# W_in split into twelve blocks, tables of two stages loaded a stage ahead, and four buffers for turned choices

## The chip, the cores and the metric

One core of one Trainium2 chip. The metric is the device time of the kernel in microseconds. A core has TensorE (PE in the profile; its weight loads are PEld), VectorE (DVE), ScalarE (ACT), GpSimd (POOL) and SyncE (SP), which here issues nearly all transfers. The engines run their own instruction streams and meet at semaphores. A transfer that SP issues is worked off by the core's 16 DMA engines.

## What is computed

One layer: a long convolution with a gate and a residual, a layer norm, a layer of experts with a residual, and another layer norm, over 8192 positions of 512 features, in float32.

```python
u = x @ W_in + b_in                       # 8192 x 1536
uc = _short_conv(u, short_w, short_b)     # three taps along the sequence
x0, x1, v = jnp.split(uc, 3, axis=-1)
v = v * x1
k = _gen_filter(...)                      # h = sin(..sin(pe @ W1)..W2), k = (h @ W3 + b3) * decay
v = _causal_fft_conv(v, k, filter_bias)   # length 16384, by Fourier transforms
y = v * x0
x = _layernorm(x + y @ W_out + b_out)
# experts: in each group of 32 positions every expert takes the position with the largest logit
perm = (logits == max over the group)     # logits = x @ controller + tie
inner = relu(x[perm] @ f1 + bias);  out = scatter(inner @ f2)
x = _layernorm(x + out)
```

## The kernel before

The program is four stages, one after the other (`program`, L1534; the list at L1531). Each stage makes its own buffers and semaphores, and its engines start together after the engines of the stage before have all ended; SP ends a stage by waiting for all of that stage's stores (L244 to L248, L643, L920 to L924), since the next stage reads them from memory.

A product that must be exact to float32 is made of three products: each operand is split into a high part (a cast to float32r, `split_high`, L77) and a low part (the rest, `split_low`, L82), and `product` (L87) multiplies high with high, low with high and high with low. W_in, x, W3, the filter's spectrum, y and W_out are treated so.

**Front stage** (`front_phase`, L113). x is worked in 17 groups along the sequence: a halo group of 256 columns (group 0), then 16 of 512. For each group TensorE runs twelve units (`unit`, L261), one for each block of 128 of the 1536 columns of W_in, in the order x0, x1, v of feature block 0, then of block 1, and so on (`w = x % 3 * DT + x // 3`). A unit is twelve matmuls into one of three PSUM buffers. ACT copies a unit's end as the halo of the next group (`keep_halo`, L350) and applies the third tap (`tap`, L357), DVE adds the other taps (`taps_add`, L465), gates and damps v (`gate`, L484) and makes the filter's angles (`angles`, L448); TensorE turns v (L280) and transforms it along one axis (`stage`, L287) in between. SP's queue begins with the whole of W_in (L193, 3 MB), the halo group of x (L194), six constants (L195 to L200), twelve parameters of the filter (L203 to L206), four position and transform tables (L209, L210), and the second group of x (L211), for which it waits until x's first split is done. ACT splits W_in in four instructions (L394), then x (L396); DVE makes W_in's low part in four (L427), POOL x's (L252). TensorE waits for all four low parts of W_in (L320), runs group 0, then waits for the constants and the parameters (L323, L324) and runs the other groups.

**Frequency stage** (`frequency_phase`, L524), 64 pairs of rows. SP loads nine tables (L614 to L623), then pairs 0 to 3 (`load`, L589), then writes the split table of ones to memory as six stores (L628) and reads it back a pair at a time (`load_ones`, L599, two pairs ahead). For each pair TensorE transforms v (L650) two pairs ahead, the filter's basis (L661) one pair ahead, makes the filter (L672) and the inverse (L684) of the pair two behind. DVE multiplies, POOL adds, ACT copies. TensorE begins when four tables are there (L648), its first filter when W3 is split (L703).

**Output stage** (`output_phase`, L787), 64 tiles of 128 positions. SP loads tile 0 (z and its transform, x0), then eight tables (L900 to L908, W_out among them), x of tile 0, and tiles 1 and 2. All of TensorE, ACT, DVE and POOL wait for the eight tables (L941, L1002, L1062, L929), then ACT and DVE split W_out (L1043, L1119), for which TensorE waits (L986). A tile is a convolution's last step (`conv`, L943), the gate, the product with W_out (`out`, L954), the norm, and the logits of 128 experts' slots (L970). At the end comes a tail: DVE marks the chosen positions in eight units (`choose`, L1108), TensorE turns them in sixteen (`turn_take`, L977), ACT writes each turned unit twice with a mask, once for each of two sides (`keep_took`, L1028), into one of two buffers, and SP stores sixteen of those (TOOK) and eight of the unturned (TAKE, L887).

**Experts' stage** (`experts_phase`, L1136): not touched.

## Time and profile before

| | us |
|---|---|
| device time, median of three runs | 2304.3 (2299.67 to 2306.85) |
| own time of the profiled execution | 2312.54 |
| its span | 2310.7 |
| TensorE busy | 1933.4 (84% of the span) |
| DVE, ACT, POOL busy | 1387.6, 949.0, 440.1 |
| moved by the DMA engines | 522.65 MB, 226 GB/s |

The profile is of one execution, which took 2312.54 us; it has the span from the first to the last instruction, and all times in it are counted from the span's start. The stages begin at about 2, 784, 1154 and 1613 us. A busy share is an average over stages with different limits, so it says little by itself. "Idle before" is time in which an engine stood ahead of an instruction, with what ended it.

### The profile page before, as it was taken

Reading aid. Unit: us, or ns where it says so; the run is one execution under the profiler, and the core shown is the slowest. Engines: PE = TensorE matmul, PEld = TensorE weight load, DVE = VectorE, ACT = ScalarE, POOL = GpSimd, SP = SyncE. Lnnn points to the kernel's source line nnn. Section 1 sums busy time; section 2 is a strip of 40 time slices with the busy share of each in tenths; the row PEclk is TensorE's granted clock in tenths of the full one; section 3 lists DMA queues with packets and bytes.
Section 4 is the critical chain, followed back from the end, with each engine's and each line's share of the span. In section 5 each row is a group of like instructions: output and inputs, shape, how many; then the busy total and the mean of one; then the engine's idle time right before and its main releaser. Section 6 shows DMA issues by size and latency. Waiting matters only on the chain. (4 is left out here: it accounts for less than half of the span.)

```text
span 2310.7 us, 35055 instructions
## 1 busy us (share of the span) xinstructions
PE 1933.4 (84%) x12598; PEld 1322.0 (57%) x12598; DVE 1387.6 (60%) x2672; ACT 949.0 (41%) x1756; POOL 440.1 (19%) x279
## 2 busy tenths in 40 slices
PE   5999999999999699999769999994767676576444
PEld 5777777777777344444359988883636362252000
DVE  3878777777777255555458888882443354354344
ACT  3444444444444344444345555554323232242222
POOL 1100010011000044444345554540000000000000
PEclk9999999999999799999979999996888887686655
DMA  4134233423332578888587777756797999989999
GB/s 144 65 110 136 102 110 110 142 101 110 117 130 92 174 202 222 221 220 223 160 258 239 243 245 225 238 185 240 251 398 270 393 345 407 406 302 409 372 392 341
DMA packets 300365, 522.65 MB, mean 226 GB/s; under 512 B 26943, under 2 KB 119263, under 8 KB 291874
## 3 DMA queue, kind: packets, MB, share of 16 engines
q1 hardware_dynamic: 290978, 503.63, 64.5%
q10 hardware_dynamic: 9216, 16.78, 1.9%
q8 instruction: 103, 1.69, 0.3%
q14 instruction: 68, 0.56, 0.1%
HBM read 314.50 MB, written 205.82 MB: 225 GB/s over the span
## 5 line engine op out<-in xcount | busy, mean ns | idle before, releaser
L89 PE MATMUL p_pu<-p_xT_high,p_win_high 128*128 128x512 f32 (+1 forms) x816 | 334.6, 410 | 23.7 <-POOL p_xT_low L84 23.5
L91 PE MATMUL p_pu<-p_xT_low,p_win_high 128*128 128x512 f32 (+1 forms) x816 | 318.3, 390 | 0.0
L90 PE MATMUL p_pu<-p_xT_high,p_win_low 128*128 128x512 f32 (+1 forms) x816 | 318.3, 390 | 0.0
L369 ACT ACTIVATE p_t<-p_pu,p_tbias,p_taps 128x512 f32<-128x512 f32 x192 | 149.4, 778 | 385.2 <-PE p_pu L91 384.1
L473 DVE SCALAR_TENSOR_TENSOR p_t<-p_halo,p_taps,p_t 128x128 f32<-128x128 f32 (+1 forms) x384 | 196.8, 517 | 137.0 <-ACT p_t L369 135.9
L473 DVE SCALAR_TENSOR_TENSOR p_t<-p_pu,p_taps,p_t 128x384 f32<-128x384 f32 (+1 forms) x384 | 210.2, 547 | 6.9
L751 POOL TENSOR_TENSOR q_y<-q_y 128x512 f32<-128x512 f32 x128 | 160.3, 1273 | 277.8 <-DVE q_y L778 277.8
L84 POOL TENSOR_TENSOR p_xT_low<-p_xT,p_xT_high 128x2048 fp32r<-128x2048 f32 (+1 forms) x17 | 77.2, 4541 | 626.0 <-ACT p_xT_high L79 626.0
L89 PEld LDWEIGHTS p_pu<-p_xT_high,p_win_high 128*128 128x128 f32 x816 | 155.0, 190 | 56.9 <-issue 29.4
L1427 DVE COPY e_taken<-e_pd 128x1024 f32<-128x1024 f32 x64 | 78.4, 1224 | 161.8 <-PE e_pd L1360 161.6
L91 PEld LDWEIGHTS p_pu<-p_xT_low,p_win_high 128*128 128x128 f32 x816 | 154.4, 189 | 34.6
L1372 PE MATMUL e_pd<-e_taken,e_ff 128*32 128x128 f32 x2048 | 90.0, 333 | 96.6 <-DMA e_ff<-in_L_ffn_f 93.0
L90 PEld LDWEIGHTS p_pu<-p_xT_high,p_win_low 128*128 128x128 f32 x816 | 155.1, 190 | 27.5
L778 DVE TENSOR_TENSOR q_y<-q_pg,q_v 128x512 f32<-128x512 f32 x256 | 157.9, 673 | 1.9 <-PE q_pg L682 1.8
L1372 PEld LDWEIGHTS e_pd<-e_taken,e_ff 128*32 128x32 f32 x2048 | 67.2, 133 | 159.8 <-DMA e_ff<-in_L_ffn_f 146.3
L1360 PE MATMUL e_pd<-e_pick,e_out 64*128 64x128 f32 x1536 | 111.0, 310 | 56.8 <-DMA e_out<-s_X 30.4
L950 PE MATMUL o_pc<-o_idft,o_zin 128*128 128x128 f32 x1024 | 127.2, 279 | 26.1 <-DVE o_wout_low L84 26.1
L1360 PEld LDWEIGHTS e_pd<-e_pick,e_out 64*128 64x128 f32 x1536 | 107.0, 222 | 66.8 <-issue 34.0
L1434 ACT COPY e_out<-e_pd 128x1024 f32<-128x1024 f32 x64 | 64.7, 1011 | 192.6 <-PE e_pd L1384 192.6
L657 PE MATMUL q_pv<-q_av,q_fwd 128*64 128x512 f32 x512 | 126.3, 616 | 15.7 <-DMA q_ah<-s_SH 15.7
L950 PEld LDWEIGHTS o_pc<-o_idft,o_zin 128*128 128x128 f32 x1024 | 122.0, 195 | 27.0 <-issue 26.9
L296 PE MATMUL p_ps<-p_vt,p_dft 128*128 128x512 f32 x256 | 134.6, 608 | 0.7 <-ACT p_vt L379 0.7
(120 smaller groups left out, 3499.9 us busy)
## 6 DMA issues: line engine op xcount, KB each, us to landing
s_I<-e_out SPq DMA_DIRECT2D x64, 1024.0 KB, 8.2
s_SV<-p_sout SPq DMA_DIRECT2D x128, 256.0 KB, 2.0
q_av<-s_SV SPq DMA_DIRECT2D x64, 512.0 KB, 4.3
s_Z<-q_z SPq DMA_DIRECT2D x128, 256.0 KB, 3.2
o_zin<-s_Z SPq DMA_DIRECT2D x64, 512.0 KB, 3.6
e_ff<-in_L_ffn_f SPq DMA_DIRECT2D x64, 512.0 KB, 8.9
e_inter<-s_I SPq DMA_DIRECT2D x32, 1024.0 KB, 12.8
e_taken<-s_I SPq DMA_DIRECT2D x32, 1024.0 KB, 11.3
```

What stands on the lines that cost most here:

```text
L89: pe.matmul(out, a[0], b[0], start=start, stop=False)
L90: pe.matmul(out, a[1], b[0], start=False, stop=False)
L91: return pe.matmul(out, a[0], b[1], start=False, stop=stop)
L296: pe.matmul(pz[n % 2][:], dft[i % 2][:, j, r, :], vt[i % 2][:, j, :], start=True, stop=True).then_inc(s_ps, 1)
L369: nc.scalar.activation(t[r][m % 2][:], pu[(W + n) % 3][:], ACT.Identity, bias=tbias[:, w:w + 1], scale=taps[:, w, 2:3]).then_inc(t_ok, 1)
L473: return dve.scalar_tensor_tensor(T[:, c], src, taps[:, w, tap:tap + 1], T[:, c], ALU.mult, ALU.add)
L657: m = pe.matmul(pv[r][a * B:(a + 1) * B, :], fwd[:, 1 if 2 * p + a else 0, r * B:(r + 1) * B], av[s][:, a, :], start=True, stop=True)
L751: pool.tensor_tensor(y[p % NY][:, r, :], y[p % NY][:, r, :], y2[p % NT2][:, r, :], (ALU.subtract, ALU.add)[r]).then_inc(y_ok, 1)
L778: dve.tensor_tensor(into, pg[k % NG][:], v[p % NV][:, half, :], ALU.mult).then_inc(g_used, 1)
L950: m = pe.matmul(pc[n % 2][:, k, :], zin[s][:, r, k * P:(k + 1) * P], idft[s][:, r, :], start=(r == 0), stop=(r == 1))
L1360: m = pe.matmul(pd[:, b, h, k].rearrange("p e g -> p g e"), x[r, a, k * P:(k + 1) * P], chosen[r, a, :].rearrange("p (g e) -> p g e", g=2) ...
L1372: m = pe.matmul(ph[s][r, :], ff[w][:, 0, k * P + e * EF:k * P + (e + 1) * EF], rows[:, k, 4 * i + e, :], start=(k == 0), stop=(k == DT - 1))
```

## The change

- `front_tables` and `output_tables` are new: buffers that live over two stages. `program` opens the first ahead of the front stage and the second ahead of the frequency stage, and hands them on.
- W_in is loaded as twelve blocks of 128 columns, in the order of the units, behind the halo group of x; the second group of x follows, then all that stood before. ACT and DVE split it block by block, ACT four blocks ahead of the halo it copies; each unit of group 0 waits for its own block's low part. The unsplit blocks share their memory with a halo buffer and the two buffers of turned v.
- The nine tables of the frequency stage are loaded in the front stage ahead of its main loop, split by ACT in group 14 and by DVE in group 15; the ones are stored by SP after its work of group 15. The frequency stage starts with pair 0 and the ones of pair 0.
- The eight tables of the output stage are loaded in the frequency stage after pair 16; ACT makes W_out's high part in four pieces at pairs 32 to 35, POOL its low part at pairs 33 to 36. The output stage starts with its tiles and waits for no table.
- Turned choices have four buffers. ACT writes the one side, DVE the other (each has a semaphore), DVE between its `choose` instructions.

The diff, cut:

```diff
@@ front_phase @@
+        shared = sb("shared", [P, W * HC + 2 * J * D])
+        halo = [sb("halo0", [P, W, HC])[:], shared[:, 0:W * HC].rearrange("p (w c) -> p w c", w=W)]
+        vt = [shared[:, W * HC + s * J * D:W * HC + (s + 1) * J * D].rearrange("p (j d) -> p j d", j=J) for s in range(2)]
+        win = [shared[:, x * DT * P:(x + 1) * DT * P].rearrange("p (k c) -> p k c", k=DT) for x in range(W)]
...
-            sp.dma_start(win[:], A["W_in"].rearrange("(k p) w -> p k w", p=P)).then_inc(w_in, 16)
+            wd = A["W_in"].rearrange("(k p) w -> p k w", p=P)
             load_x(0)
+            for x in range(W):
+                sp.dma_start(win[x], wd[:, :, at(x)]).then_inc(w_in[x], 16)
+            load_x(1)
             sp.dma_start(taps[:], A["short_w"].rearrange("(w p) k -> p w k", p=P)).then_inc(consts, 16)
...
-            load_x(1)
+            sp.dma_start(ones[:], A["ones"]).then_inc(fw_in, 16)
+            for r in range(2):
+                sp.dma_start(w_raw[0][r * HID:(r + 1) * HID, :], A["W3"]).then_inc(fw_in, 16)
...
+            sp.dma_start(F["fwd"][:], A["fwd"]).then_inc(carried, 16)
...
+                if i == NCH - 1:
+                    sp.wait_ge(ones_low, ONE + 1)
+                    for n, part in enumerate((0, 0, 1)):
+                        for a in range(2):
+                            sp.dma_start(S["ONES"][n, :, :, a, :], F["ones"][part][a * HID:(a + 1) * HID].bitcast(F32)
+                                         .rearrange("p (r b) -> p r b", r=3)).then_inc(ones_st, 16)
...
+                if g == 0:
+                    pe.wait_ge(w_low, ONE + x + 1)
...
-            pe.wait_ge(w_low, ONE + DT)
...
-            act.wait_ge(w_in, ONE + 16)
-            for c in range(DT):
-                split_high(nc.scalar.copy, win_s[0][:, c, :], win[:, c, :]).then_inc(w_high, 1)
+            def high_w(x):
+                act.wait_ge(w_in[x], ONE + 16)
+                split_high(nc.scalar.copy, win_s[0][:, :, at(x)], win[x]).then_inc(w_high, 1)
+
             high(0)
+            for x in range(4):
+                high_w(x)
             for x in range(W):
                 if x == 6:
                     high(1)
+                if x + 4 < W:
+                    high_w(x + 4)
...
             for i in range(NCH + 1):
+                if i == NCH - 2:
+                    act.wait_ge(fw_in, ONE + 80)
+                    split_high(nc.scalar.copy, F["ones"][0][:], ones[:]).then_inc(ones_high, 1)
+                    split_high(nc.scalar.copy, F["w_a"][:], w_raw[0][:]).then_inc(fw_high, 1)
+                    split_high(nc.scalar.copy, F["w_b"][:], w_raw[1][0:HID + 3, :]).then_inc(fw_high, 1)
@@ frequency_phase @@
-            for p in range(NA):
+            for p in range(2):
                 load(p)
-            sp.wait_ge(ones_high, ONE + 1)
-            sp.wait_ge(ones_ok, ONE + 1)
...
+                load_ones(p)
+            for p in range(2, NA):
+                load(p)
...
+                if p == PAIRS // 4:
+                    sp.dma_start(wout[:], A["W_out"].rearrange("(k p) d -> p k d", p=P)).then_inc(w_in, 16)
+                    sp.dma_start(O["grow"][:], A["grow"]).then_inc(carried, 16)
...
             for p in range(-2, PAIRS + LAG):
+                if PAIRS // 2 <= p < PAIRS // 2 + DT:
+                    k = p - PAIRS // 2
+                    act.wait_ge(w_in, ONE + 16)
+                    split_high(nc.scalar.copy, O["wout"][0][:, k, :], wout[:, k, :]).then_inc(w_high, 1)
...
             for p in range(PAIRS):
+                if PAIRS // 2 < p <= PAIRS // 2 + DT:
+                    k = p - PAIRS // 2 - 1
+                    pool.wait_ge(w_high, ONE + k + 1)
+                    split_low(pool, O["wout"][1][:, k, :], wout[:, k, :], O["wout"][0][:, k, :]).then_inc(w_low, 1)
@@ output_phase @@
-            pe.wait_ge(consts, ONE + 16 * NCONST)
...
-            pe.wait_ge(w_low, ONE + 1)
...
+            def keep_took(v):
+                dve.wait_ge(took_ok[0], ONE + v + 1)
+                if v >= NK:
+                    dve.wait_ge(took_st[v % NK], ONE + v // NK * 16)
+                dve.tensor_scalar(took[v % NK][:, :, :, 1, :], pt[v % 2][:].rearrange("p b (h e) -> p b h e", h=2),
+                                  side[:, 1:2], None, ALU.mult).then_inc(took_ok[1], 1)
...
                 for u in chosen(n):
                     choose(u)
+                    if u > UNITS:
+                        for b in range(2):
+                            keep_took(2 * (u - UNITS - 1) + b)
+            for b in range(2):
+                keep_took(2 * UNITS - 2 + b)
```

## Rows read from the trace of the kernel before

**Rows 1.** Windows: stretch, length, busy PE, PEld, DVE, ACT, POOL, PEclk, DMA share, GB/s.

```profile
90.00:700.00 610.00, 610.00 (x2655) 458.93 (x2653) 478.99 (x969) 280.18 (x525) 60.51 (x14) 1.00 0.33 114
...
830.00:1130.00 300.00, 300.00 (x1344) 128.45 (x1342) 156.86 (x280) 143.79 (x280) 140.22 (x112) 1.00 0.81 219
...
1210.00:1370.00 160.00, 160.00 (x1073) 144.40 (x1072) 132.59 (x269) 91.01 (x215) 85.30 (x54) 1.00 0.78 244
```

**Rows 2.** TensorE's waits: us in total, times, longest.

```profile
PE o_pt L983 <- ACT o_took L1033: 15.5, 13, 2.6
```

**Rows 3.** Timeline of the start, all engines: start us, us, engine, line, operation.

```profile
2.36 0.44 SPq L193 DMA_DIRECT2D p_win<-in_L_attn_W_in  x1
...
3.95 8.94 SPq L196 DMA_DIRECT2D p_bin<-in_L_attn_b_in  x1
...
18.36 1.04 ACT L79 CAST p_xT_high<-p_xT 128x1024 fp32r<-128x1024 f32 x1
...
19.48 3.85 POOL L84 TENSOR_TENSOR p_xT_low<-p_xT,p_xT_high 128x1024 fp32r<-128x1024 f32 x1 [19.05 <-ACT p_xT_high L79]
...
21.05 2.31 DVE L432 TENSOR_TENSOR p_tsum<-p_taps 128x12 f32<-128x12 f32 x1
...
23.48 0.55 PE L89 MATMUL p_pu<-p_xT_high,p_win_high 128*128 128x256 f32 x1 [23.48 <-POOL p_xT_low L84]
...
36.77 4.61 POOL L84 TENSOR_TENSOR p_xT_low<-p_xT,p_xT_high 128x2048 fp32r<-128x2048 f32 x1 [13.44 <-ACT p_xT_high L79]
...
45.89 0.78 ACT L369 ACTIVATE p_t<-p_pu,p_tbias,p_taps 128x512 f32<-128x512 f32 x1 [2.49 <-PE p_pu L91]
```

**Rows 4.** Transfers: KB each, median us from issue to landing.

```profile
p_xT<-in_L_attn_xT SPq DMA_DIRECT2D x16, 1024.0 KB, 6.5
...
o_x<-s_X SPq DMA_DIRECT2D x64, 256.0 KB, 4.3
...
q_ones<-in_ones SPq DMA_DIRECT2D x1, 96.0 KB, 2.1
```

**Rows 5.** Timeline of the frequency stage's start.

```profile
784.65 0.33 SPq L614 DMA_DIRECT2D q_ones<-in_ones  x1
...
788.86 0.62 ACT L79 CAST q_w_a<-q_w_raw 128x512 fp32r<-128x512 f32 x1 [1.69 <-DMA q_w_raw<-in_L_attn_b]
...
789.16 0.43 SPq L594 DMA_DIRECT2D q_av<-s_SV  x1
...
790.03 0.69 DVE L84 TENSOR_TENSOR q_w_a<-q_w_raw,q_w_a 64x512 fp32r<-64x512 f32 x1 [2.47 <-ACT q_w_b L79]
...
794.65 6.24 PE L657 MATMUL q_pv<-q_av,q_fwd 128*64 128x512 f32 x16 [15.72 <-DMA q_ah<-s_SH]
```

**Rows 6.** Timeline in the front stage's group 15, DVE and TensorE.

```profile
726.17 1.13 DVE L473 SCALAR_TENSOR_TENSOR p_t<-p_pu,p_taps,p_t 128x384 f32<-128x384 f32 x2
...
730.23 0.58 PE L89 MATMUL p_pu<-p_xT_high,p_win_high 128*128 128x512 f32 x1
```

**Rows 7.** Timeline in the frequency stage, SP and TensorE.

```profile
906.97 1.09 SPq L611 DMA_DIRECT2D s_Z<-q_z  x2
...
908.78 0.92 SPq L594 DMA_DIRECT2D q_av<-s_SV  x1
...
916.51 1.08 PE L657 MATMUL q_pv<-q_av,q_fwd 128*64 128x512 f32 x4
```

**Rows 8.** Timeline of the output stage's start.

```profile
1154.49 0.39 SPq L865 DMA_DIRECT2D o_zin<-s_Z  x1
...
1168.97 1.90 ACT L79 CAST o_wout_high<-o_wout 128x2048 fp32r<-128x2048 f32 x1 [20.50 <-DMA o_ident<-in_ident]
...
1173.48 6.34 PE L950 MATMUL o_pc<-o_idft,o_zin 128*128 128x128 f32 x32 [26.09 <-DVE o_wout_low L84]
```

**Rows 9.** Windows of 3 us in the tail, columns as in rows 1.

```profile
1594.00:1597.00 3.00, 1.09 (x4) 0.72 (x4) 0.00 (x0) 1.74 (x4) 0.00 (x0) 0.50 0.39 140
...
1600.00:1603.00 3.00, 1.49 (x7) 0.79 (x5) 0.00 (x0) 2.12 (x4) 0.00 (x0) 0.50 0.99 373
```

More of the change, by code:

```diff
@@ L814, in output_phase @@
                for s in range(2)]
-        wout_s = [ctx.enter_context(nc.sbuf_tensor(f"o_wout_{n}", [P, DT, D], F32R)) for n in ("high", "low")]
         stats = [sb(f"stats{s}", [P, 6]) for s in range(2)]
@@ L821, in output_phase @@
         top = [sb(f"top{s}", [P, UG]) for s in range(2)]
-        took = [sb(f"took{s}", [P, 4, 2, 2, ES // 2]) for s in range(2)]
-        side = sb("side", [P, 2])
+        took = [sb(f"took{s}", [P, 4, 2, 2, ES // 2]) for s in range(NK)]
         pc = [ps(f"pc{s}", [P, DT, P]) for s in range(2)]
@@ L892, in store_unit @@
                     v = 2 * u + b
-                    sp.wait_ge(took_ok, ONE + v + 1)
-                    sp.dma_start(td[v], took[v % 2][:].rearrange("p b h g e -> p b (h g e)")).then_inc(took_st[v % 2], 16)
+                    for s in range(2):
+                        sp.wait_ge(took_ok[s], ONE + v + 1)
+                    sp.dma_start(td[v], took[v % NK][:].rearrange("p b h g e -> p b (h g e)")).then_inc(took_st[v % NK], 16)
             for n in range(NZ):
@@ L979, in turn_take @@
                 if v >= 2:
-                    pe.wait_ge(took_ok, ONE + v - 1)
+                    for s in range(2):
+                        pe.wait_ge(took_ok[s], ONE + v - 1)
                 for b in range(4):
@@ L1528, in _, with program, run @@
             scale(NT - 1)
-PHASES = [front_phase, frequency_phase, output_phase, experts_phase]
-def program(nc, A, S, phases=None):
-    for phase in phases or PHASES:
+def program(nc, A, S):
+    def run(phase, *tables):
         with ExitStack() as ctx:
-            phase(nc, Semaphores(ctx, nc), A, S)
+            phase(nc, Semaphores(ctx, nc), A, S, *tables)
+    with ExitStack() as made:
+        F = front_tables(made, nc)
+        run(front_phase, F)
+        O = output_tables(made, nc)
+        run(frequency_phase, F, O)
+        run(output_phase, O)
+    run(experts_phase)
 def constants():
```

166 lines of the change are left out of this document (74 added, 92 removed).

## The prediction, made before the changed kernel had run

> **What bounds the kernel now.** I read the windows by stretch first, because the four stages have different limits. In the front stage TensorE is busy for 610.00 of 610.00 us, in the frequency stage for 300.00 of 300.00, in the output stage for 160.00 of 160.00, each at the full granted clock of 2.4 GHz [rows 1]. Whatever starts such a stage earlier moves all that follows; whatever delays TensorE once inside it is lost. The change does not touch the experts' stage, which only starts earlier.
>
> Then TensorE's waits. Three lie ahead of stages, and the rows of the timeline that end them name what came last: 23.48 us at the start, for POOL's low part of x [rows 3]; 15.72 ahead of the frequency stage, for a load [rows 5]; 26.09 ahead of the output stage, for DVE's low part of W_out [rows 8]. A fourth is 15.5 in pieces in the tail, for ACT's copies of turned choices [rows 2]. These the change can reach.
>
> **The change part by part.** Durations are from the one profiled execution: span 2310.7, own time 2312.54 us, which is 8.2 over the median of 2304.3. The sum is a difference and is applied to both.
>
> *1. Start.* Before: x is issued behind the 3 MB of W_in; ACT splits x at 18.36, POOL takes 3.85 more, and the first matmul is at 23.48 [rows 3]. After: x goes first. A small table alone in the queue landed 2.1 us after its issue [rows 4]. The 512 KB of x are 1.7 us more at the 313 GB/s below, and I give a cold queue 0.3: issued at 2.4, it lands at 6.5. ACT's 1.04 ends at 7.6, POOL's 3.85 at 11.4, first matmul at 11.5: **12 us earlier**. If POOL took half of its 4.61 us for 128x2048 [rows 3], it would be 13.5.
>
> Do the twelve blocks keep up? A block has 512-byte rows, as the output stage's loads of x0 have (256 KB, median landing 4.3 us) [rows 4], and that stage moves 244 GB/s at a share of 0.78 [rows 1]: 313 GB/s when full, 0.84 us a block. Block n lands near 6.5+0.84(n+1), the last at 16.6. TensorE needed 19.6 us for the twelve units of the halo group (23.48 to about 43.1, where unit 0 of group 1 begins, 2.8 ahead of its tap at 45.89 [rows 3]), so it asks for the last block after 29. ACT splits block x+4 before it copies halo x, so it is four units ahead.
>
> Group 1 waits for more: x's second group, the six constants and the twelve filter parameters, all now behind W_in in SP's queue. That queue blocks when much is outstanding: before, the issue of b_in hung 8.94 us behind W_in, x and the taps [rows 3]. After: x's second group is issued at 12 (it waits for POOL), lands by 20, and ACT takes it at its sixth halo, near 23; POOL's 4.61 ends by 29.5. The taps are, I estimate, let in at 16 and the other constants by 20; the twelve parameters take 6 us at the 0.5 of a table's issue (nine from 784.65 to 789.16 [rows 5]) and land at 28. TensorE gets there at 11.5+19.6=31.1, 3 us later. I keep 12; the low end is 7, if the queue blocks eight us more.
>
> In the trace DVE's addition of 12 columns takes 2.31 us, just until POOL's split ends [rows 3]. The Trainium skill (SBUF — State Buffer, on the shared port) says that a DVE operation with two SBUF inputs and a GpSimd one shut each other out for a whole instruction. By that, POOL could need only half of 4.61 where DVE is idle; the row agrees, and the start would come 13.5 earlier. I stay at 12, since DVE will be splitting blocks then.
>
> *2. Tables of the frequency stage carried by the front stage.* Nine loads (SP some 4.5 us) stand ahead of the third load of x, which ACT wants 20 us later: nothing. ACT's three splits, at most 0.62 each [rows 5], delay one tap of group 14 by 1.9 us, DVE's three, at most 0.69 [rows 5], the chain of group 15 by 2.1. At the tightest place TensorE starts a unit at 730.23 whose buffer DVE released at 727.30 (726.17+1.13) [rows 6]: 2.9 us of slack, so nothing; without that cover each would cost its 1.9 or 2.1. SP's six stores of ONES (some 4 us of issue) go out in the last group, where TensorE waits for no store.
>
> What it removes: SP issues nine tables (784.65 to 789.16) and then pair 0; TensorE starts at 794.65, 5.5 us after pair 0's issue [rows 5]. After, pair 0 is issued at 784.65: **4.5 us**, and 0.7 more (between 0 and 1.5) for 0.9 MB less ahead of it in the queue: **5.2**. The filters, 9.5 us into the stage, then find ONES landed.
>
> *3. Tables of the output stage loaded at pair 16.* Eight loads, 2.0 MB: 4 us of SP, and 6.8 us of DMA at 300 GB/s, where the share is already 0.81 [rows 1]. In steady state SP stores Z at 906.97 and loads a pair from 908.78 that is first used at 916.51 [rows 7]. Put the store at 0: the batch is issued from 1.7, its packets run from about 4 to 11; the next pair's 640 KB take 2.1 behind it and land at 13.1; they are needed at 9.5. **A loss of 3 us**, once, since TensorE is then late itself and the next pair in time. Bounds: 0, if the queue's gaps absorb it, and 6.8, all of it.
> ACT's four splits of a quarter of 1.90 [rows 8] and POOL's four of a quarter of 4.61 [rows 3] fall one to a pair of 5.4 us, in which both engines are busy for half [rows 1]: nothing, as the inverse wants POOL's result only two pairs later; without that, 1.2 a pair.
>
> *4. Output stage.* SP issues tile 0 at 1154.49 and eight tables behind it; ACT starts at 1168.97 when the last has landed, splits for 1.90, DVE after it, TensorE at 1173.48 [rows 8]. After, the first convolution needs tile 0's 640 KB alone: 1154.5+2.1+2.1+0.3=1159.0: **14.5 us**. Tile 1 is wanted 3.2 later (half of 6.34 [rows 8]) and is 1.2 MB behind, 3.8: up to 0.6 is given back. Bounds 11 and 15.5.
>
> *5. Tail.* Sixteen TOOK and eight TAKE stores, 12.6 MB. A full window runs at 373 GB/s, one at 140 [rows 9]. At 375 the bytes take 33.5 us; now they take some 35.7. Four buffers and two engines remove ACT's waits for stores, not the bytes: 2.2, less 0.7 for the start: **1.5 us**; bounds 0 and 3.
>
> **Sum**: -12 -5.2 +3 -14.5 -1.5 = **-30.2 us**: 2282.3 for the profiled execution, 2274.1 for the median. A difference under 0.3% (7 us) can't be told from none here.
>
> **The rivals.**
> A. The parameters gate group 1. SP's queue stays blocked on the taps' many small descriptors; the 8.94 us of b_in [rows 3] speak for it. The first matmul is at 11.5, but TensorE stands ahead of group 1, and the start gains 6: 2280.1.
> B. The output stage's gap is ruled by transfers. Three tiles of 1.2 MB are wanted at once, and x0 and x of tile 0 lie between tiles. If TensorE gets them no faster than they came before, 8 us are won for 14.5: 2280.6. Against: tile 0 was issued first before too.
> C. The batch at pair 16 starves more pairs than one, as the share of 0.81 leaves little to catch up with [rows 1]: 10 us for 3: 2281.1.
> D. Slower. The twelve blocks don't overlap, and each takes a landing of x0's, 4.3 us [rows 4]. The last lands at 6.5+51.6=58.1, x's second group 6.5 (its median [rows 4]) later at 64.6, ACT and POOL 6.5 more: 71.1 for group 1, against 43.1. That is +28.0 in place of -12, and with the rest's -18.2, 2314.1. It decides from 3.5 us a block on. Against it: 313 GB/s in a stage full of such loads.
> The Trainium skill (DMA: Bandwidth & Descriptors, Anatomy of one DMA) gives each DMA some 2.0 us fixed, and its bytes at 436 GB/s. By that, as an estimate, twelve blocks in a row are 31 us and group 1 begins 7.6 later than now. The tail's stores, one behind the other at 373 GB/s [rows 9], show the fixed parts overlapping.
> E. The tables bring nothing, as each stage first waits for the stores of the one before: only the start gains, 2292.3; or the start fails too, 2304. Against: the waits end on the tables or on what stands behind them [rows 5, 8].
>
> **Chances.** Forecast 0.62; A 0.14; B 0.10; C 0.06; D 0.03; E 0.05, of it 0.03 with no change. All low ends together (7, 4.5, -6.8, 11, 0) give -15.7, 2288.6; all high ends (13.5, 6, 0, 15.5, 3) give -38, 2266.3. So **2265 to 2289** holds the forecast with A, B and C; D and E are left out. Faster by over 0.3%: 0.94; within: 0.03; slower: 0.03.
>
> **What would show it.** First matmul near 11.5, first tap near 34, and no wait of TensorE before the frequency stage. Waits of about 10.5 us ahead of that stage and 11.5 ahead of the output stage, both on a stage's own data. One wait of some 3 us on a pair's load near pair 21. No DMA window with a gap in the tail. A wait of L89 for a constant or for x's second group means A, for blocks of W_in, D; a first convolution later than 4.5 us behind tile 0's issue means B.

## The result, and the profile after

The changed kernel took 2291.82 us (median of five runs, 2287.93 to 2293.73), the kernel before beside it 2305.12 (2299.67 to 2309.86): a ratio of 0.9938, with a 95% interval of 0.9922 to 0.9953, or 13.3 us less. The forecast was 30.2 us less, 2274.1, with a range from 2265 to 2289. The sign was right; the size was not, and the time lies outside of the range. A later comparison of the same two kernels (e_again, below) gave 2295.45 against 2307.09, 0.9950 (0.9937 to 0.9962).

The profiled execution of the changed kernel has a span of 2291.9 and its own time of 2293.73, 18.8 us under the profile of before. The profile of before lay 7.4 us over the median of 2305.12, that of the changed kernel 1.9 over its own, which makes the difference from 13.3. A second profile of the kernel before (e_before, below) has a span of 2303.7. So I read the gain stage by stage.

The windows of the changed kernel, inside the front, frequency and output stages (columns as in [rows 1]):

```profile
90.00:700.00 610.00, 610.00 (x2653) 459.38 (x2653) 479.48 (x963) 282.32 (x528) 64.25 (x14) 1.00 0.33 115
820.00:1120.00 300.00, 294.75 (x1316) 126.34 (x1314) 152.78 (x274) 142.25 (x279) 142.58 (x114) 0.99 0.81 222
1190.00:1350.00 160.00, 160.00 (x1061) 143.64 (x1061) 131.89 (x267) 90.00 (x211) 85.59 (x54) 1.00 0.77 242
```

TensorE still bounds all three. In the middle one it is idle for 5.25 of 300 us, where before it was never idle: that is the batch of tables. The third looks like the row of before and hides a loss, since an engine that is slower and always busy shows no gap.

The timeline of the start, all engines, which answers [rows 3]:

```profile
2.98 0.44 SPq L211 DMA_DIRECT2D p_xT<-in_L_attn_xT  x1
3.48 10.05 SPq L228 DMA_DIRECT2D p_shared<-in_L_attn_W_in  x12
...
8.45 2.35 POOL L84 TENSOR_TENSOR p_xT_low<-p_xT,p_xT_high 128x1024 fp32r<-128x1024 f32 x1 [8.02 <-ACT p_xT_high L79]
...
8.93 4.83 DVE L84 TENSOR_TENSOR p_win_low<-p_shared,p_win_high 128x512 fp32r<-128x512 f32 x5 [5.54 <-ACT p_win_high L79]
...
11.49 0.55 PE L89 MATMUL p_pu<-p_xT_high,p_win_high 128*128 128x256 f32 x1 [11.49 <-DVE p_win_low L84]
...
24.09 4.58 POOL L84 TENSOR_TENSOR p_xT_low<-p_xT,p_xT_high 128x2048 fp32r<-128x2048 f32 x1 [13.29 <-ACT p_xT_high L79]
...
24.56 5.26 DVE L84 TENSOR_TENSOR p_win_low<-p_shared,p_win_high 128x512 fp32r<-128x512 f32 x2 [2.53 <-ACT p_win_high L79]
...
35.27 0.78 ACT L422 ACTIVATE p_t<-p_pu,p_tbias,p_taps 128x512 f32<-128x512 f32 x1 [2.49 <-PE p_pu L91]
```

The first matmul came at 11.49, 12.0 earlier, as forecast; the first tap at 35.27 instead of 45.89, 10.6 earlier. The two rows near 24 say why: DVE's last two blocks took 5.26 us where one alone takes 0.69, for as long as POOL was splitting x's second group, and TensorE waited 1.79 us for the first of them:

```profile
29.27 0.39 PE L89 MATMUL p_pu<-p_xT_high,p_win_high 128*128 128x256 f32 x1 [1.79 <-DVE p_win_low L84]
```

The timeline from the batch at pair 16 on, SP and TensorE (answers [rows 7]), and behind it the windows of the same place:

```profile
876.11 0.99 SPq L691 DMA_DIRECT2D q_wout<-in_L_attn_W_out  x1
...
880.69 0.50 SPq L699 DMA_DIRECT2D t_ident<-in_ident  x1
881.30 0.38 SPq L658 DMA_DIRECT2D q_av<-s_SV  x1
881.72 0.47 SPq L660 DMA_DIRECT2D q_ah<-s_SH  x1
...
889.19 3.40 PE L713 MATMUL q_pv<-q_av,f_fwd 128*64 128x512 f32 x8 [5.25 <-DMA q_ah<-s_SH]
```

```profile
880.00:885.00 5.00, 3.94 (x20) 1.82 (x16) 2.81 (x5) 2.21 (x5) 2.15 (x2) 1.00 0.99 303
885.00:890.00 5.00, 0.81 (x2) 0.30 (x4) 0.00 (x0) 0.04 (x1) 1.29 (x2) 0.88 1.03 375
890.00:895.00 5.00, 5.00 (x20) 2.09 (x18) 1.33 (x3) 1.54 (x3) 0.00 (x0) 0.78 0.64 240
```

One pair's spectra landed at 889.19. TensorE had waited 5.25 us, and ran its next eight matmuls in 3.40 us instead of 1.94, since the granted clock had fallen from 1.00 towards the lower of its two levels (1.2 and 2.4 GHz) while it stood still. Of the way from pair 16 to pair 20 that makes 28.22 us instead of 21.47.

The two gaps ahead of stages (answers [rows 5] and [rows 8]):

```profile
774.21 0.37 SPq L658 DMA_DIRECT2D q_av<-s_SV  x1
778.68 1.98 PE L713 MATMUL q_pv<-q_av,f_fwd 128*64 128x512 f32 x4 [10.34 <-DMA q_ah<-s_SH]
```

```profile
1144.78 0.39 SPq L910 DMA_DIRECT2D o_zin<-s_Z  x1
...
1149.65 6.37 PE L982 MATMUL o_pc<-o_idft,o_zin 128*128 128x128 f32 x32 [12.05 <-DMA o_idft<-in_idft]
```

The wait ahead of the frequency stage fell from 15.72 to 10.34, the one ahead of the output stage from 26.09 to 12.05, each now on the stage's own data. These two parts did what was forecast.

In the tail, TensorE's wait of [rows 2] has become

```profile
PE o_pt L1016 <- DVE o_took L1136: 11.6, 10, 3.3
```

which is less, and yet the tail is as long: 47.3 us from the first choice to the experts' first matmul, 47.1 before. The gap of [rows 9] is gone, and the full windows are slower (below).

Put together, profile against profile, in us (negative is a gain; each term is the difference of two distances between the same instructions):

| part | forecast | measured |
|---|---|---|
| start, to the first tap | -12 | -10.6 |
| front's last matmul to the frequency stage's first | -5.2 | -5.4 |
| inside the frequency stage | +3 | +6.2 (+6.75 from the batch) |
| its last matmul to the output stage's first | -14.5 | -14.0 |
| output stage, first matmul to first choice | 0 | +6.7 |
| first choice to the experts' first matmul | -1.5 | +0.2 |
| experts' stage | 0 | -1.9 |
| sum | -30.2 | -18.8 |

### The profile page after: what moved, and what is told of

Its sections match the earlier page's. It is cut to its first block and busy times, and to the rows that moved or that the text cites. A ratio compares the mean times of both kernels' runs of the same rounds, so it can differ in the third digit from the quotient of the medians.

```text
span 2291.9 us, 35132 instructions
## 1 busy us (share of the span) xinstructions
PE 1934.8 (84%) x12598; PEld 1322.7 (58%) x12598; DVE 1405.0 (61%) x2695; ACT 940.8 (41%) x1751; POOL 443.1 (19%) x283
## 5 line engine op out<-in xcount | busy, mean ns | idle before, releaser
L89 PE MATMUL p_pu<-p_xT_high,p_win_high 128*128 128x512 f32 (+1 forms) x816 | 334.8, 410 | 13.5 <-DVE p_win_low L84 13.3
L91 PE MATMUL p_pu<-p_xT_low,p_win_high 128*128 128x512 f32 (+1 forms) x816 | 318.3, 390 | 0.0
L90 PE MATMUL p_pu<-p_xT_high,p_win_low 128*128 128x512 f32 (+1 forms) x816 | 318.3, 390 | 0.0
L89 PEld LDWEIGHTS p_pu<-p_xT_high,p_win_high 128*128 128x128 f32 x816 | 155.0, 190 | 46.6 <-POOL p_xT_low L84 11.5
L91 PEld LDWEIGHTS p_pu<-p_xT_low,p_win_high 128*128 128x128 f32 x816 | 154.3, 189 | 34.3
L90 PEld LDWEIGHTS p_pu<-p_xT_high,p_win_low 128*128 128x128 f32 x816 | 155.1, 190 | 27.2
L713 PE MATMUL q_pv<-q_av,f_fwd 128*64 128x512 f32 x512 | 127.3, 620 | 15.6 <-DMA q_ah<-s_SH 15.6
L536 DVE SCALAR_TENSOR_TENSOR p_t<-p_halo,p_taps,p_t 128x128 f32<-128x128 f32 x192 | 100.2, 527 | 65.0 <-ACT p_t L422 64.5
L536 DVE SCALAR_TENSOR_TENSOR p_t<-p_shared,p_taps,p_t 128x128 f32<-128x128 f32 x192 | 96.8, 508 | 69.9 <-ACT p_t L422 69.5
L84 DVE TENSOR_TENSOR q_h_b<-q_ph,q_h_a 64x256 fp32r<-64x256 f32 (+1 forms) x64 | 26.8, 418 | 178.3 <-ACT q_h_a L79 178.3
```

The costliest lines, as they stand in the source:

```text
L84: return eng.tensor_tensor(low, x, high.bitcast(F32), ALU.subtract)
L89: pe.matmul(out, a[0], b[0], start=start, stop=False)
L90: pe.matmul(out, a[1], b[0], start=False, stop=False)
L91: return pe.matmul(out, a[0], b[1], start=False, stop=stop)
L536: return dve.scalar_tensor_tensor(T[:, c], src, taps[:, w, tap:tap + 1], T[:, c], ALU.mult, ALU.add)
L713: m = pe.matmul(pv[r][a * B:(a + 1) * B, :], fwd[:, 1 if 2 * p + a else 0, r * B:(r + 1) * B], av[s][:, a, :], start=True, stop=True)
```

## The experiments

Each is an edit of the changed kernel unless it says otherwise, and each came with runs of the kernel before beside it, so ratios are to that kernel. Their intervals are some 3 to 4 us to either side, and the changed kernel itself gave 2291.82 and 2295.45; so a gain of 1 to 4 us is read from the stretch of the trace that the edit touches, and not from the time. The period is the time from one tile of the output stage to the next; the tail goes from its first choice to the experts' first matmul.

**Where buffers lie.** No trace shows addresses. They are counted here from the sizes in each kernel, with the buffers one behind the other, each at a multiple of 32 bytes, and the first at 128 modulo 256. So counted, before, every large buffer of the output stage but b_out's began at a multiple of 64; behind the carried tables (16, 8 and 4 bytes a partition among them) every one begins 32 bytes beside one. Of the address modulo 256, the loads, y and its halves went from 192 to 224, W_out's halves from 192 to 128, the buffers of turned choices from 0 to 32.

```diff
-            "side": sb("side", [P, 2]), "eps": sb("eps", [P, 1])}
+            "side": sb("side", [P, 2]), "eps": sb("eps", [P, 1]),
+            "pad": sb("pad", [P, 8])}
```

> 32 bytes of padding behind the carried output tables, nothing else: every buffer of the output stage, and the frequency stage's load and store buffers, then start at a multiple of 64 bytes, as in the kernel before, and not 32 bytes beside one. Theory (placement costs the transfers): the tail from the first choice to the experts' first issue falls from 42.4 us to 39 to 40.5, its transfers go back from about 345 GB/s to above 370, and the output stage's period falls from 6.02 us a tile to 5.98; in all 3 to 5 us under the changed kernel, 2287 to 2289. Rival (placement is nothing: the tail is bound by the waits for the stores, the period by the locks between DVE and POOL): the tail stays at 42 to 43 us, the period at 6.02, the time within 1 us of 2291.8.

Measured: 2288.99 us, ratio 0.9927 (0.9915 to 0.9940). From tile 12 to tile 36 the period went from 6.020 us to 6.003 (5.982 before). The tail did not move: 47.2 us from the first choice to the experts' first matmul (47.3 without the padding), at 357 GB/s. Half of the theory fell. But a multiple of 64 is not what the buffers had before, so the next one gave back the whole residue.

```diff
-    return {"wout": [...
+    return {"pad0": sb("pad0", [P, 16]), "wout": [...
...
+            "pad": sb("pad", [P, 40])}
```

> 64 bytes of padding ahead of the carried output tables and 160 behind: W_out's halves, the loads, y and its halves and the choices' buffers all have the address modulo 256 bytes that they had in the kernel before. 32 bytes behind alone brought the period from 6.020 to 6.002 us a tile (5.982 before) and left the tail's rate. Theory (placement of the operands): the period is 5.98 to 5.985, which is 1 us over the stage under the first padding. Rival (the remaining 0.02 has another cause, as a wait on one more semaphore): 6.00 to 6.02. For the tail: if the choices' buffers' place sets the rate it is 370 and the tail about 41; else 358 and 42.4.

Measured: 2288.14, ratio 0.9915 (0.9895 to 0.9935). The period is 5.973 us, all of the loss and a little more. The rows of the output product, 120 us of the steady part by form (busy us, mean ns), first of before, then of the changed kernel, then of e_align:

```profile
L89 PE MATMUL o_po<-o_wout_high,o_y_high 128*128 128x512 f32 x81 | 33.5, 414 | 0.0
L91 PE MATMUL o_po<-o_wout_low,o_y_high 128*128 128x512 f32 x81 | 31.9, 394 | 0.0
```

```profile
L89 PE MATMUL o_po<-t_wout_high,o_y_high 128*128 128x512 f32 x80 | 33.4, 418 | 0.0
L91 PE MATMUL o_po<-t_wout_low,o_y_high 128*128 128x512 f32 x80 | 31.8, 397 | 0.0
```

```profile
L89 PE MATMUL o_po<-t_wout_high,o_y_high 128*128 128x512 f32 x82 | 33.9, 414 | 0.0
L91 PE MATMUL o_po<-t_wout_low,o_y_high 128*128 128x512 f32 x81 | 31.8, 393 | 0.0
```

Some 3 to 4 ns more for each of a tile's twelve matmuls of this form are the 0.04 us a tile. (A second profile of the kernel before has a period of 5.977, so the two kernels differ by 0.038 to 0.043.) The tail became 45.4 us, and its full stretches move 394 GB/s. To see which buffers do it, two more kernels moved one group each:

```diff
+        sb("pad", [P, 56])
         took = [sb(f"took{s}", [P, 4, 2, 2, ES // 2]) for s in range(NK)]
```

> The changed kernel with 224 bytes of padding just ahead of the four buffers of turned choices, so that they alone start at a multiple of 256 bytes; all else stays 32 beside. Theory (the place of the stored buffers sets the rate of the tail's transfers): the full stretches go from 358 to 390 to 397 GB/s and the tail, from the first choice to the first copy of the experts' stage, from 49.5 us to 47.6 as with all residues of before; the period of the output stage stays at 6.02; about 2290. Rival (the residues of the operands or of the logits matter too): the rate stays below 375 and the tail above 48.5.

```diff
-    return {"wout": [...
+    return {"pad0": sb("pad0", [P, 16]), "wout": [...
...
+            "pad": sb("pad", [P, 48])}
```

> The changed kernel with 64 bytes of padding ahead of the carried output tables and 192 behind: W_out's halves alone (with the controller, growth tables and the identity) get the residue modulo 256 that they had before; loads, y and its halves and the choices keep theirs. Theory 1 (PE's reads of W_out, the moving operand, depend on its place): the period falls from 6.020 us a tile to between 5.98 and 6.00. Theory 2 (it is the place of y, its halves or of what the transfers write, and W_out's does nothing): the period stays at 6.015 to 6.02. In both the tail stays at 49.5.

e_took: 2287.55, ratio 0.9923 (0.9906 to 0.9939). Windows of 12 us, from 12 us behind the first choice on, of before, the changed kernel, and e_took:

```profile
1583.31:1595.31 12.00, 5.40 (x21) 3.54 (x22) 0.00 (x0) 6.28 (x10) 0.00 (x0) 0.50 0.88 324
```

```profile
1566.14:1578.14 12.00, 5.17 (x20) 3.58 (x20) 6.58 (x10) 3.44 (x5) 0.00 (x0) 0.50 1.03 357
```

```profile
1560.69:1572.69 12.00, 6.52 (x24) 4.29 (x24) 7.65 (x12) 3.53 (x6) 0.00 (x0) 0.50 1.07 394
```

The place of the stored buffers alone makes 394 GB/s of 357, and the tail 45.0 us (1548.69 to 1593.71); the period stays at 6.019. The Trainium skill (DMA: Bandwidth & Descriptors, How a descriptor splits into AXI transactions) says that transactions begin at 256-byte boundaries, so that the first one of a descriptor that starts beside one begins at the boundary below and fetches bytes that it does not use. For these rows of 1 KB that is, as an estimate by that page, five transactions for four. The measured direction agrees; that residue 64 (e_pad) was as slow as 32 agrees too. By the page's count of beats it would be 33 for 32, or 3%; the runs show 10% in these windows, and 6% if each rate is divided by its DMA share (368 against 347 GB/s).

e_wout: 2289.17, 0.9936 (0.9919 to 0.9954); the period is 6.009, between what its two theories expected, the tail 47.6. W_out's place gives 0.011 of the 0.047 us, the first padding gave 0.017; both together give more than their sum, so the operands' places are not independent. The profiles sort by one thing: where W_out's halves and y's have the same residue (192 in the kernel before, e_align, e_all and e_most, 0 in e_256) the period is 5.973 to 5.982, where they differ (128 and 224, 192 and 224, 128 and 0) 6.003 to 6.020. No run was made to test this, so whether it is the rule, and what in the chip would cause it, stays open.

**The number of buffers for turned choices.** `NK` is 2, then 8, for 4.

> The changed kernel with two buffers for the turned choices instead of four; ACT and DVE still copy half each. Its tail is 42.4 us from the first choice to the experts' first issue, with the DMA engines full at about 358 GB/s for 28 us; the kernel before had 42.2 us with a gap, but 370 GB/s where they were full. Theory (four stores in flight move less per us than two): the full stretches go back to 370 to 375 GB/s, and the tail is 41 to 42.5 us. Rival 1 (the rate comes from where the buffers lie or from how they are written): the full stretches stay at 355 to 360, gaps come back, and the tail is 43.5 to 45. Rival 2 (the tail is bound by bytes alone at one rate): as with four, 42.4.

> The changed kernel with eight buffers for the turned choices. Theory (more stores in flight, less per us): 340 to 350 GB/s, tail 43 to 44.5 us. Rival (only the gaps count, and with four none is left): as with four, 358 GB/s and 42.4 us.

e_nk2: 2292.07, 0.9928 (0.9911 to 0.9944), tail 49.9 us at 338 GB/s, with the DMA share down to 0.93: the gaps came back, as its rival 1 said. e_nk8: 2288.07, 0.9917 (0.9896 to 0.9938), tail 47.3 at the rate of four buffers. The theory of too many stores in flight fell. At equal placement four buffers are worth 2.5 us over two, and the forecast of 1.5 was sound: with the stored buffers at their old residue the tail falls from 47.1 us before to 45.0, by 2.1.

**The batch of tables.**

```diff
-                if p == PAIRS // 4:
-                    ... (eight loads)
+                if 0 <= p - PAIRS // 4 < len(late):
+                    dst, src, got = late[p - PAIRS // 4]
+                    sp.dma_start(dst, src).then_inc(got, 16)
```

> The batch of eight tables at pair 16 goes out one transfer a pair, W_out in four pieces, from pair 16 to 26. Theory (the batch starves PE once: 5.25 us of waiting for a pair's spectra plus 1.5 us of matmuls at half clock): the one wait for a pair's spectra goes, no matmul of the stage's middle runs at half clock, and the stage is 6 to 7 us shorter; 2285 to 2286. Rival (the engines behind had slack that swallowed the hit, or each single transfer holds a pair up by 0.5 us): the wait goes but the stage is less than 2 us shorter, 2290 to 2292.

Measured: 2284.58, 0.9914 (0.9899 to 0.9928). TensorE has no wait for a pair's spectra in the middle of the stage, and from pair 16 to pair 20 it takes 21.4 us again. The whole hit goes, 6.8 us. (In the ten other profiles with the batch in one piece the wait was 4.10 to 5.22 us.) The windows of the same place in e_spread, to be held against those above:

```profile
880.00:885.00 5.00, 5.00 (x24) 2.15 (x22) 2.81 (x5) 2.21 (x6) 2.15 (x3) 1.00 0.87 276
885.00:890.00 5.00, 5.00 (x24) 2.15 (x22) 2.72 (x5) 2.21 (x5) 2.15 (x3) 1.00 0.96 277
```

```diff
+                if p == PAIRS // 4 + 4:
+                    sp.dma_start(wout[:], ...).then_inc(w_in, 16)
                 if p == PAIRS // 4:
-                    sp.dma_start(wout[:], ...).then_inc(w_in, 16)
```

> The batch at pair 16 is split in two: its seven small tables (1 MB together) at pair 16, W_out (1 MB) alone at pair 20. Theory (a backlog of bytes: a megabyte fits into what the queue has to spare before a pair's spectra are late, two do not): the wait of 5.25 us at pair 20 goes or falls under 1 us at each of the two places, and the half clock with it; 5 to 6.7 us gained. Rival 1 (SP's eight issues one behind the other are what delays the next pair's): the wait stays at 3 us or more at the first place and none is at the second. Rival 2 (each megabyte starves PE by itself): two waits of 2 to 3 us, no gain.

Measured (one run, 2285.62): two waits, and no half clock behind either.

```profile
888.91 1.94 PE L714 MATMUL q_pv<-q_av,f_fwd 128*64 128x512 f32 x8 [2.82 <-DMA q_ah<-s_SH]
...
911.67 1.94 PE L714 MATMUL q_pv<-q_av,f_fwd 128*64 128x512 f32 x8 [1.25 <-DMA q_ah<-s_SH]
```

Seven issues with 1 MB cost 2.82 us, one issue with 1 MB cost 1.25. So the bytes count, and something of the seven loads besides: the theory that one megabyte fits fell, and so did both rivals in part. SP's time is the likely one (4.0 us from the first of the seven to the next pair's load, against 1.1), but the seven also have other forms, some with a few bytes a row, and this one run does not separate the two.

**DVE and POOL at the start.** The second x group is split after W_in's last block.

```diff
-                if x == 6:
-                    high(1)
                 if x + 4 < W:
                     high_w(x + 4)
+                if x == 8:
+                    high(1)
```

> ACT splits the second x group after the last of W_in's twelve blocks (at the ninth unit instead of the seventh), so POOL's split of it, 4.58 us, starts when DVE has done its last two blocks. Theory (DVE is locked out while POOL reads and writes: its last two block splits took 5.26 us for two instead of 0.69 each, and PE waited 1.9 us for the eleventh): the wait of PE for the eleventh block goes, the first tap starts at 33 to 34 us instead of 35.27, and the kernel is 1.3 to 2 us faster, about 2290. Rival (the second group then comes late: PE waits as long for its low part as it did for the block): the first tap stays at 35 to 35.5, no difference.

Measured: 2289.29, 0.9933 (0.9921 to 0.9946); first tap at 34.59, 0.7 earlier: between the two. Of this the edit gives some 0.3: TensorE's one wait is 1.47 us instead of 1.79, and the clock rose 0.35 earlier in this execution (14.65 for 15.00), which is not the edit's. The blocks are no longer late, but now the group is (timeline of e_start, DVE, POOL and TensorE):

```profile
26.62 4.59 DVE L495 TENSOR_TENSOR p_tsum<-p_taps 128x12 f32<-128x12 f32 x1 [2.09 <-DMA p_ident<-in_ident]
...
26.60 4.58 POOL L84 TENSOR_TENSOR p_xT_low<-p_xT,p_xT_high 128x2048 fp32r<-128x2048 f32 x1 [16.20 <-ACT p_xT_high L79]
...
31.45 0.47 PE L89 MATMUL p_pu<-p_xT_high,p_win_high 128*128 128x512 f32 x1 [1.47 <-POOL p_xT_low L84]
```

DVE's sum of 12 columns, 0.17 us by itself, took 4.59 beside POOL's 4.58. The Trainium skill (SBUF — State Buffer, Terms) calls the pair of ports that these two engines share exclusive, "held for the full instruction"; the row agrees.

The wait costs more than itself. Twelve profiles have the unedited start, and all of them this wait of 1.8 us. In five (the changed kernel's first, e_took, e_pad, e_spread, e_outstart) the granted clock stays at its upper level behind it, and the first tap comes at 35.14 to 35.93. In the seven others it falls to the lower level, within 1 us of the wait's end and for some 3.2 us, and the first tap comes at 37.20 to 37.90. The windows behind the wait, of the changed kernel and then of e_again, which has the same code:

```profile
29.00:32.00 3.00, 2.73 (x23) 2.73 (x24) 1.51 (x7) 0.37 (x1) 0.00 (x0) 1.00 0.66 181
32.00:35.00 3.00, 3.00 (x16) 2.29 (x14) 0.19 (x1) 0.37 (x1) 0.00 (x0) 1.00 1.01 343
```

```profile
29.00:32.00 3.00, 2.34 (x12) 2.34 (x13) 1.90 (x7) 0.00 (x0) 0.06 (x1) 0.65 0.79 243
32.00:35.00 3.00, 3.00 (x18) 2.87 (x18) 0.19 (x1) 0.74 (x2) 0.00 (x0) 0.78 1.03 316
```

In e_all, e_most and e_256 (below), where DVE makes both low parts and TensorE has no such wait, the clock does not fall, and the first tap comes at 33.20 to 34.15, though it rose at 14.8 to 17.5 as elsewhere.

**The output stage's start.** POOL waits for tile 0's low part before it makes the second gate and the first sums.

```diff
+                if n == 0:
+                    pool.wait_ge(y_low, ONE + 1)
+                    continue
+                for m in range(0 if n == 1 else n, n + 1):
...
```

> At the start of the output stage POOL waits, after the first gate, until DVE has split tile 0's y, and adds the bias of tiles 0 and 1 after the second gate. Theory (POOL's first gates and sums stretch DVE's first chain from 0.69 to 1.33, 1.63 and 1.41 us, PE idles 3.33 us for it, and its first output product then runs at half clock): the three take 0.69 to 0.78 each, PE's first output product starts about 2.2 us earlier after its first inverse product (9.7 us apart now, 7.5 then) and the gain at tile 10 is 2.5 to 4.5 us; 2287.5 to 2289.5. Rival (tile 1's gate comes late instead, and the transfers of tiles 2 and 3 set the pace of the start): the first product is earlier but tile 4 starts as before, less than 1 us gained.

Measured: 2291.34, 0.9939 (0.9927 to 0.9952). The first output product comes 7.39 us after the first inverse one, not 9.70, but tile 1's gate is then late, and 1.3 us are left at the first choice. Even these are not shown: from the stage's first matmul to the first choice it takes 403.16 us, in four profiles with the unedited start (the changed kernel, e_again, e_experts, e_spread) 404.4 to 404.5, and in five others with that start and the same period (e_took, e_nk2, e_start, e_late, e_nk8) 401.75 to 402.62. So the mechanism is shown, and that this edit gains is not. In the changed kernel the chain of tile 0 reads (DVE's timeline, where 0.69 is the undisturbed time of each):

```profile
1154.20 1.33 DVE L1097 TENSOR_TENSOR o_y<-o_y,o_gate 128x512 f32<-128x512 f32 x1
1155.57 1.63 DVE L1100 TENSOR_TENSOR o_y<-o_y,o_offs 128x512 f32<-128x512 f32 x1
1157.88 1.41 DVE L84 TENSOR_TENSOR o_y_low<-o_y,o_y_high 128x512 fp32r<-128x512 f32 x1 [0.68 <-ACT o_y_high L79]
```

and TensorE behind it, first in the changed kernel, then in e_pad, whose start is the same code:

```profile
1159.35 0.79 PE L89 MATMUL o_po<-t_wout_high,o_y_high 128*128 128x512 f32 x1 [3.33 <-DVE o_y_low L84]
1159.94 0.63 PE L90 MATMUL o_po<-t_wout_high,o_y_low 128*128 128x512 f32 x1
```

```profile
1158.42 0.50 PE L89 MATMUL o_po<-t_wout_high,o_y_high 128*128 128x512 f32 x1 [1.71 <-DVE o_y_low L84]
1158.76 0.39 PE L90 MATMUL o_po<-t_wout_high,o_y_low 128*128 128x512 f32 x1
```

The first ran at the lower level after 3.33 us of idleness, the second at the upper. Tile 2 came 11.6 to 11.9 us behind tile 0 in four profiles (the changed kernel's first and e_again among them) and 9.2 to 10.7 in eight others with the same start; in before it was 8.95. In the four, TensorE was idle for 3.00 to 3.33 us and its next ten matmuls of the product ran at the lower level. But 3.42 us (e_align) were followed by no fall, and 1.85 (e_nk2) by one. So some 2 us of this are a matter of the execution.

**Both kernels once more.**

> The kernel before, unchanged, for a second profiled execution. The first lies 7 to 8 us above the median of its runs, so that the two profiles differ by 18.8 us where the medians differ by 13.3. Theory (the difference lies in the experts' stage, whose transfers vary): its first stages stand as in the first profile within 1 us each (first tap 45.9, 320 us from the frequency stage's first PE operation to the output stage's, minus what starts the clock), the experts' stage is 3 to 7 us shorter than 692. Rival (the first profile has its excess in the stages that the change touches, at the start above all): the first tap at 43 to 44, and the changed kernel's start brings less than 10.6 us.

> The changed kernel, unchanged, for a second profiled execution. In thirteen profiles of kernels whose start is the same code the first tap comes at 35.1 to 37.9 us, by when the first group's matmuls go from half to full clock (14.6 to 17.5). Theory (this moment differs from execution to execution, and is no part of the change): first tap between 35 and 38, the single wait for a pair's spectra again 4.5 to 5.5 us, period 6.02, tail 47.3 us to the experts' first PE operation, 2288 to 2293. Rival: start or tail outside of these.

e_before gave 2305.41 us against 2307.09, 0.9996 (0.9986 to 1.0006). Its first tap is at 45.48; its frequency stage is 2.0 us shorter than in the first profile and its experts' stage 688.9 instead of 692.3: the theory holds for half of the 7 us, and the frequency stage has the rest. e_again is the 2295.45 of the beginning, 2.5 over the upper end that was expected. Its first tap is at 37.20, its wait at the batch 4.72 us, its experts' stage 696.3. Between these two profiles the start's gain is 8.3 us and not 10.6.

**What can be had.** First the parts above together, with two refinements: DVE, and not POOL, makes the second x group's low part behind its blocks, and POOL makes each sum behind the next gate.

> The parts that the runs so far support, together: the batch spread over eleven pairs; the second x group split after W_in's last block, and its low part made by DVE behind its own blocks (no lock: POOL's 4.58 us held DVE's next operation for 4.59); POOL's first bias sums put behind the split of tile 0's y and each sum behind the next gate; the padding of the run before. Theory (the parts add up): start 2 to 2.5 us under the changed kernel (first tap at 33 to 33.5), 6.5 in the frequency stage, 2 to 4 at the output's start, 1.5 to 2 in its period: 12 to 15 us under 2291.8, so 2277 to 2280. Rival (they overlap, or the clock's phase at the output's start is lost again): 2281 to 2285.

Measured: 2276.26, ratio 0.9861 (0.9844 to 0.9877), 15.6 us under the changed kernel; by their medians the four parts alone gave 7.2 (batch), 3.7 (places), 2.5 (start) and 0.5 (output's start). The last three lie within the intervals. Here the first tap is at 34.15. Then the padding where the change had not been:

```diff
+        sb("pad0", [P, 32])
         taken = sb("taken", [P, DT * EH * GH])
...
+        sb("pad1", [P, 24])
         inter = ...
```

> The changed kernel with 224 bytes of padding in the experts' stage, which the change did not touch: its loads, its outputs and the buffers that they are stored from start at multiples of 256 bytes instead of 32 beside one. From its first issue to the end it takes 695.3 us, with a DMA share of 0.84 to 1.03 in every stretch. Theory (the residue sets the rate, as 358 against 397 GB/s in the output tail, wherever the engines are full): its full stretches rise by up to a tenth, and the stage is 10 to 60 us shorter, 2232 to 2282. Rival (loads into SBUF and packets of 2 KB do not feel it as the stores of 1 KB did): within 3 us of 695.

Measured: 2277.17, ratio 0.9883 (0.9866 to 0.9899); the stage takes 677.3 us (675.6 and 676.1 in e_most and e_256), where the fifteen profiles with its old placement gave 686.4 to 696.3. Three of its windows of 100 us, in the changed kernel and then in e_experts:

```profile
1610.00:1710.00 100.00, 67.02 (x1032) 46.82 (x1028) 38.78 (x45) 27.38 (x28) 0.00 (x0) 0.86 0.84 309
...
1910.00:2010.00 100.00, 56.82 (x636) 29.71 (x638) 37.29 (x71) 26.04 (x34) 0.00 (x0) 0.75 1.04 404
...
2110.00:2210.00 100.00, 49.19 (x312) 10.46 (x304) 38.26 (x95) 24.64 (x40) 0.00 (x0) 0.57 1.01 384
```

```profile
1610.00:1710.00 100.00, 68.56 (x1074) 48.25 (x1074) 41.53 (x46) 29.35 (x29) 0.00 (x0) 0.88 0.87 326
...
1910.00:2010.00 100.00, 62.74 (x697) 34.80 (x696) 41.58 (x73) 28.20 (x37) 0.00 (x0) 0.74 1.04 412
...
2110.00:2210.00 100.00, 46.76 (x280) 8.64 (x280) 39.34 (x99) 25.00 (x41) 0.00 (x0) 0.57 1.02 392
```

At an equal share the rate is 1 to 2% higher where the share is full: less than the 6% of the 1 KB stores, but over 690 us it is worth as much as the whole change.

> The kernel of all supported parts (2276.3 us) with the experts' padding and, in the front and frequency stages, padding that puts their loads and stores on multiples of 256 bytes too. Theory: what the experts' padding alone gives is added in full; the front and frequency stages, whose transfers share is 0.33 and 0.82 and whose PE is always busy, keep 5.36 us a pair and give less than 2 us. Rival (PE reads its operands faster at some places): a pair falls below 5.33 us, 2 to 4 us more.

> As the fastest kernel so far (2258.7 us), but with nearly all large buffers of all stages at multiples of 256 bytes: W_out's halves, the loads, y and its halves too, which there have the residue 192 that they had before. Theory (multiples of 256 are best throughout): the output stage's period falls from 5.972 us a tile to 5.95 to 5.97, and the rest is the same, 2256 to 2259. Rival (any multiple of 64, alike for all operands, does as well): period 5.97, 2257 to 2261.

e_most: 2258.73, 0.9799 (0.9784 to 0.9813). e_256: 2255.65 against 2307.09, 0.9774 (0.9757 to 0.9791). The output stage's period is the same in both, 5.973: here the rival holds. But e_256 is shorter in the front stage, from the first tap to the last matmul 726.3 us, against 732.8 in the changed kernel and 731.0 in e_most: W_in's halves, at residue 128 in both of these, are at 0 there, and so are the tables ahead of them. Its product takes 416, 390 and 393 ns by line (L89 to L91), in e_most 416, 394 and 394, in the changed kernel 418, 396 and 396. This is one profile, and W_in's halves were not moved alone.

## Why the prediction was right and wrong

- *Start (item 1).* "First matmul at 11.5" was right to 0.01, by luck: ACT began x's split at 7.33 and not 6.5, POOL took 2.35 us and not 3.85, and DVE's first block, which had to wait for POOL, added its 0.69. "I keep 12" failed behind it. The item named DVE's block splits only as a reason for POOL's slowness, and did not ask who waits for DVE when POOL's 4.6 us fall among them: TensorE does, 1.8 us, of which 1.4 are left at the first tap of the first profile. In seven of twelve profiles the clock fell behind this wait, for some 3.2 us, which costs about half of that more, and a later first rise (14.6 to 17.5 us in the profiles of this start) the rest. The first taps lie from 35.14 to 37.90.
- *Rivals A, B, D and E* did not happen: the constants and parameters were issued by 29 us and nothing waited for them; the blocks of W_in landed 0.9 us apart (ACT starts to split them at 9.11, 10.01, 10.91), where D needed 3.5; both gaps closed as computed. The fixed part that D's last sentences take from the Trainium skill (DMA: Bandwidth & Descriptors, Anatomy of one DMA) is given there for transfers that GpSimd issues, and these are SP's.
- *Frequency tables (item 2).* Right: 5.4 for 5.2, and nothing lost in groups 14 and 15, as the cover named there said (front's last matmul at 10.6 earlier, as its first tap).
- *The batch (item 3).* Right in place and kind, one wait near pair 21 as written, and wrong in size. "They land at 13.1, needed at 9.5" gave 3; it measured 5.25 of wait and 1.5 of matmuls at the lower clock, 6.75 in all, which is the item's upper bound. The spectra landed 14.8 us after the store, not 13.1: the sum went by the packets' bytes alone. SP's eight issues put the pair's load 5.2 us behind the batch's first, and e_late shows that seven loads cost more than one of the same bytes. And no term was there for what the clock takes after a wait. Rival C, several pairs starved, did not happen.
- *Output stage's gap (item 4).* Right: 14.0 for 14.5. "Up to 0.6 is given back", the next sentence, was the error: it looked at transfers alone. The wait for tables had covered POOL's first gates and sums. With the cover gone they ran beside DVE's first chain. That is 2.3 us on the first product in the first profile, and up to 2.3 more where the clock then fell.
- *Tail (item 5).* The mechanism was right and is worth 2.1, but all of it was taken back by where the buffers had come to lie.
- *What no item had.* The change moved tables ahead of other buffers, and with them every address behind: 2.0 us over the output stage by its period, and 2.3 in the tail. It was costed at nothing without being named.

Of the 17 us between the forecast and the medians' 13.3, the runs so account for 3.75 (batch), 1.4 to 3.7 (start), 2.3 to 4.5 (output's start) and 4 (placement), 11.5 to 16; the rest is within what two executions differ by in the experts' stage alone.

## What to carry to other kernels

A change that makes buffers live longer also moves the address of every buffer behind them: compare these modulo 256 before and after, and compare the mean of an always busy engine's instructions, since a loss there shows no gap. Where a wait is taken away, list what every engine did under its cover, pairs that share a port above all, and not just the transfers. A batch of loads in a loop whose DMA share is 0.8 goes in one piece a turn; all at once it costs the time by which the next turn's data are late, and the clock behind the wait. A short wait of TensorE can cost its length again, since the granted clock may fall behind it: judge a start from several profiles.

## What was not expected of the hardware

- 1 KB stores from buffers counted to lie at a multiple of 256 bytes ran at 394 GB/s, from 32 or 64 bytes beside one at 357, with the DMA engines full in both (shares of 1.07 and 1.03).
- A matmul of 128x512 took 390 or 395 ns (L90, in e_256 and in the changed kernel) by where its operands lay.
- The same start reached the upper clock between 14.6 and 17.5 us, and fell from it behind an idle time of 1.8 us in seven of twelve profiles. In the output stage an idle time of 1.85 us (e_nk2) was followed by a fall, one of 3.42 (e_align) was not.
